# Third norm and router as one stage: half-wise choices, 16-bit places, shared down projection in the last stage

## The reference

```python
logits = x @ gate_weight.T                    # x: the normed tokens, 64 experts
scores = softmax(logits)
# the 3 best of 8 groups (by their maximum) stay, then the 6 best experts of a token
topk_w, topk_i = top_k(masked scores, 6)
# place of a choice in its expert = how many earlier choices took that expert
slot = flat * 96 + minimum(pos, 95)           # 96 places; late ones overwrite place 95
buf = zeros.at[slot].set(x[tok])              # rows gathered per expert
out = silu(buf @ Wg) * (buf @ Wu) @ Wd        # 64 experts, M = 176
y = sum of a token's 6 rows, weighted by topk_w
shared = silu(x @ Sg.T) * (x @ Su.T) @ Sd.T   # all tokens, MS = 352
result = residual + y + shared
```

## Time and profile before

| | before |
|---|---|
| median of 3 runs | 1584.75 us (1584.71 to 1588.64) |
| profiled execution | 1592.02 us, its span 1590.2 us |
| TensorE busy | 1389.2 us (87%) |
| VectorE busy | 1122.2 us (71%) |
| ScalarE busy | 677.8 us (43%) |
| GpSimd busy | 736.8 us (46%) |
| mean granted TensorE clock | 0.926 of 2.4 GHz |

### The profile page before, as it was taken

The page is one execution under the profiler, slowest core; times in us unless marked ns, Lnnn a source line. Parts: engine busy times, 40 slices in busy tenths (PEclk is TensorE's granted clock), DMA queues, the critical chain, the costliest instruction groups (busy, mean ns, idle before and its releaser), DMA issues. The chain is left out here.

```text
span 1590.2 us, 35116 instructions
## 1 busy us (share of the span) xinstructions
PE 1389.2 (87%) x13733; PEld 973.9 (61%) x13733; DVE 1122.2 (71%) x2131; ACT 677.8 (43%) x1430; POOL 736.8 (46%) x811
## 2 busy tenths in 40 slices
PE   3859999998669999999999999999986986799942
PEld 2424555555536777777777777777765545688831
DVE  4767888885767888888788888887864579122229
ACT  1226777772135555555555555555551110122200
POOL 0341111100228787666667666766650026577710
PEclk9968999999779999999999999999997698899965
DMA  3052000000016888798788878887882500599948
GB/s 107 1 221 98 2 2 2 2 2 1 29 59 137 155 153 146 136 159 142 143 141 155 149 138 143 155 145 138 147 144 76 175 1 3 172 291 286 269 128 267
DMA packets 423541, 191.57 MB, mean 120 GB/s; under 512 B 377506, under 2 KB 397696, under 8 KB 423248
## 3 DMA queue, kind: packets, MB, share of 16 engines
q1 hardware_dynamic: 404576, 164.08, 49.1%
q0 software_dynamic: 6144, 12.52, 2.8%
q10 hardware_dynamic: 12656, 12.72, 2.5%
HBM read 73.91 MB, written 23.13 MB: 61 GB/s over the span
## 5 line engine op out<-in xcount | busy, mean ns | idle before, releaser
L945 POOL CAST a_ph<-a_p 128x1024 f16<-128x1024 f32 (+7 forms) x256 | 247.6, 968 | 233.3 <-ACT a_p L1091 232.0
L1141 DVE TENSOR_TENSOR a_ph<-a_p,a_ph 128x1024 f16<-128x1024 f32 (+7 forms) x256 | 260.2, 1016 | 14.5 <-POOL a_ph L945 14.4
L1091 ACT ACTIVATE a_p<-bank,a_negm 128x1024 f32<-128x1024 f32 (+7 forms) x256 | 189.1, 739 | 124.8 <-DVE a_negm L1158 124.4
L1051 PE MATMUL bank<-a_v,a_pt 128*128 128x128 f16 x3456 | 234.7, 219 | 6.0 <-DMA a_pt<-a_ph 6.0
L1033 PE MATMUL bank<-a_k,a_q 128*128 128x512 f16 (+3 forms) x1152 | 229.1, 326 | 7.9 <-ACT a_p L1091 7.9
L1051 PEld LDWEIGHTS bank<-a_v,a_pt 128*128 128x128 f16 x3456 | 211.0, 98 | 37.0 <-issue 5.7
L1158 DVE TENSOR_REDUCE a_negm<-bank 128x1 f32<-128x1024 f32 (+7 forms) x256 | 189.8, 742 | 24.7 <-PE bank L1038 23.0
L976 PE MATMUL bank<-x_part,wsplit 128*128 128x512 f16 x768 | 189.1, 383 | 1.9 <-PEq L185 1.8
L690 ACT ACTIVATE a_p<-bank 128x1024 f32<-128x1024 f32 x192 | 153.0, 810 | 68.5 <-PE bank L575 57.6
L1033 PEld LDWEIGHTS bank<-a_k,a_q 128*128 128x128 f16 x1152 | 98.8, 98 | 69.3 <-ACT a_p L1091 8.9
L710 DVE TENSOR_REDUCE a_max<-bank 128x2 f32<-128x1024 f32 (+3 forms) x128 | 128.7, 1021 | 17.4 <-PE bank L575 14.9
(11 more groups left out here) (206 smaller groups left out, 2452.4 us busy)
## 6 DMA issues: line engine op xcount, KB each, us to landing
wgu<-in_wgu SPq DMA_DIRECT2D x64, 352.0 KB
choice_rows<-zero SPq DMA_DIRECT2D x24, 512.0 KB, 5.8
wh<-in_wqkv SPq DMA_DIRECT2D x32, 384.0 KB, 4.0
c_rows<-choice_rows ACTq DMA_DIRECT2D x16, 768.0 KB
wd<-in_wd SPq DMA_DIRECT2D x64, 176.0 KB
a_pt<-a_ph SPq DMA_TRANSPOSE x256, 3.8
x<-in_x SPq DMA_DIRECT2D x1, 2048.0 KB, 8.7
wo<-in_wo SPq DMA_DIRECT2D x1, 2048.0 KB, 10.0
```

The source lines that it names most:

```text
L945: pool.tensor_copy(halves[j][:, :, 0, :], probs[j % 2][:, 0:blocks[j] * P].rearrange("p (n q) -> p n q", q=P)).then_inc(h_ready, 1)
L1051: ins = pe.matmul(V_ps[j % 2][:, 0:DH1], turned[j][:, 2 * q + a, :], vs[n % 2][v_][:, q, :], start=(q == 0 and (a, v_) == PARTS[0]), stop= ...
L1091: act.activation(probs[j % 2][:, 0:w_], S_ps[j % 2].rearrange("p a n -> p (a n)")[:, 0:w_], ACT.Exp, bias=negm[:, n % 2, j:j + 1], accum_o ...
L1141: dve.tensor_tensor(halves[j][:, :, 1, :], probs[j % 2][:, 0:blocks[j] * P].rearrange("p (n q) -> p n q", q=P), halves[j][:, :, 0, :], ALU ...
```

## The change

The block of norm n3 is gone; its work is in the router block. TensorE turns two tiles, then logits and turns alternate (`logit(p)`, `turn(p)`); ScalarE alone copies to `xT`. The small loads are issued before the stores of `xn`, the weights behind them. `tmp`, `sc`, `msc` and `sg` lie in the memory of `xn`, so VectorE waits for the stores (`s_kept`) ahead of the softmax. Softmax, groups and choices run for 8 tiles at a time, on scores that are not yet divided by their sum. Tables of choices and places are f16 (`oh`, `mask`, `cm`, `posh`, `prod`, `fin`, `vh`); ScalarE copies the places to SBUF and makes the second half of `at_expert`; the running sum goes by groups of four tiles, finished by extra matmuls. Place 95 is no longer clipped but added by 16 small matmuls of `fin`. The gate and up steps 9 to 11 lie between the first picks. The shared down projection and its sum run in `combine`, in the same PSUM group as the rows of place 95.

```diff
-        with ExitStack() as c1:
-            g.xn = g.sb("xn", [P, NT, D], F32, c)
-            norm(nc, g, "n3", "keep")
...
+            for q in range(4):
+                sp.wait_ge(s_xn, 4 * q + 4)
+                sp.dma_start(xv[:, 4 * q:4 * q + 4, :], xn[:, 4 * q:4 * q + 4, :]).then_inc(s_kept, 16)
...
+            turn(0)
+            turn(1)
             pe.wait_ge(s_in, 80)
...
+            for p in range(NT // 2):
+                logit(p)
+                if p + 2 < NT // 2:
+                    turn(p + 2)
...
+            for n in range(9):
                 gate_up(n)
...
+            places()
+            gate_up(9)
+            pick(0)
+            gate_up(10)
+            pick(1)
+            gate_up(11)
+            pick(2)
+            pe.wait_ge(s_h, len(gu_steps))
             pe.wait_ge(s_wov, 1)
...
+            pick(3)
+
+            pe.wait_ge(s_fin, 1)
+            for t in range(NT):
+                pe.matmul(g.bank[0][0:C, 1, 0:E], lastcol[:, :], fin[:, t, :], start=False, stop=False)
+            pick(4)
+            pick(5)
...
+            for h in range(2):
+                act.wait_ge(s_sub, h + 1)
+                act.activation(sc[:, h * HT:h * HT + HT, :], tmp[:, h * HT:h * HT + HT, :], ACT.Exp).then_inc(s_ex, 1)
...
+            dve.wait_ge(s_kept, 64)
+            shifted(0)
+            groups(0)
+            choices(0)
+            shifted(1)
+            shared(1)
+            groups(1)
+            shared(2)
+            choices(1)
+            shared(3)
+            eid = iotah[:, 0:E].unsqueeze(1).to_broadcast([P, NT, E])
+            for k in range(K):
+                dve.tensor_tensor(oh[:, k], eid, gih[:, :, k:k + 1].to_broadcast([P, NT, E]),
+                                  ALU.is_equal).then_inc(s_oh, 1)
+                dve.wait_ge(s_oh, k + 1)
+                if k:
+                    chained(dve.tensor_tensor(mask[:, :, :], oh[:, 0] if k == 1 else mask[:, :, :], oh[:, k], ALU.add))
+                shared(min(4 + k, 7))
...
+            def slots(k):
+                if k == 0:
+                    dve.wait_ge(s_posh, 2)
+                chained(dve.tensor_tensor(prod[:, :, :], posh[:, :, :], oh[:, k], ALU.mult))
+                chained(dve.tensor_reduce(v[:, k, :], prod[:, :, :], AX.X, ALU.add))
+                chained(dve.tensor_copy(vh[:, k, :], v[:, k, :]))
+                if k >= 2:
+
+                    dve.wait_ge(s_used, k - 1)
+                dve.tensor_tensor(ph[k % 2][:, :, :], iotah[:, :].unsqueeze(1).to_broadcast([P, NT, C]),
+                                  vh[:, k, :].unsqueeze(2).to_broadcast([P, NT, C]), ALU.is_equal).then_inc(s_ph, 1)
...
-                shared_sum(2 * k)
-                shared_sum(2 * k + 1)
...
+            shared(10)
+            slots(1)
+            shared(11)
+            slots(2)
+            shared(12)
+            dve.wait_ge(s_sel, 1)
+            dve.scalar_tensor_tensor(msc[:, :, :], pos, C - 1.5, sc[:, :, :], ALU.is_gt,
+                                     ALU.mult).then_inc(s_wov, 1)
+            slots(3)
+            slots(4)
+            slots(5)
...
-                pool.tensor_scalar(eh[k % 2][:, :, 1, :], oh[:, k], float(k + 1), None, ALU.mult).then_inc(s_eh, 1)
...
+                for m in range(NMS):
+                    w_ = SM[m][1]
+                    pe.matmul(b_, g.hT[0:w_, m, t * P:(t + 1) * P], g.sd[0:w_, m, :], start=(m == 0), stop=False)
+                if t == 0:
+                    pe.wait_ge(s_l, 16)
+                pe.matmul(b_, g.wovT[:, t * P:(t + 1) * P], last[:, :], start=False, stop=True).then_inc(s_mm, 1)
```

More of the change, by code:

```diff
@@ new lines, in pick @@
+            def pick(k):
+                pe.wait_ge(s_e0, k + 1)
+                pe.wait_ge(s_e1, k + 1)
+                pe.wait_ge(s_ph, k + 1)
+                for t in range(NT):
+                    ins = pe.matmul(g.bank[0][0:C, 1, 0:2 * E], ph[k % 2][:, t, :],
+                                    eh[k % NEH][:, t, :, :].rearrange("p a e -> p (a e)"),
+                                    start=(k == 0 and t == 0), stop=(k == K - 1 and t == NT - 1))
+                ins.then_inc(s_used, 1)
@@ L1529, in shared @@
                     done += 1
+            for t in range(NT):
+                dve.bn_aggr(mv[:, t, :], g.stats[:, t, :]).then_inc(s_ag, 1)
+            dve.wait_ge(s_ag, NT)
+            chained(dve.tensor_copy(g.mean[:, :], mv[:, :, 0]))
+            chained(dve.tensor_copy(t1[:, :], mv[:, :, 1]))
+            chained(dve.tensor_scalar(ve[:, :], t1[:, :], EPS, None, ALU.add))
+            dve.wait_ge(s_sq, 1)
+            chained(dve.reciprocal(sq[:, :], sq[:, :]))
+            chained(dve.tensor_tensor(t1[:, :], sq[:, :], sq[:, :], ALU.mult))
@@ L1531, in _ @@
+            chained(dve.tensor_tensor(t1[:, :], t1[:, :], ve[:, :], ALU.mult))
+            chained(dve.tensor_scalar(t1[:, :], t1[:, :], -0.5, 1.5, ALU.mult, ALU.add))
+            chained(dve.tensor_tensor(g.rstd[:, :], sq[:, :], t1[:, :], ALU.mult))
+            for t in range(NT):
+                dve.tensor_scalar(xn[:, t, :], g.x[:, t, :], g.mean[:, t:t + 1], g.rstd[:, t:t + 1],
+                                  ALU.subtract, ALU.mult).then_inc(s_xn, 1)
             dve.wait_ge(s_in, 80)
[L1532 removed]
@@ new lines, in _ @@
+            slots(0)
+            dve.wait_ge(s_pos, 3)
+            chained(dve.tensor_scalar(cnt[:, :], count, -1.0, None, ALU.add))
+            chained(dve.tensor_tensor(fin[:, :, :], posh[:, :, :], cnt[:, :].unsqueeze(1).to_broadcast([P, NT, E]),
+                                      ALU.is_equal))
+            dve.nop().then_inc(s_eq, 1)
+            shared(10)
[6 more added lines that the diff above has]
+                                     ALU.mult).then_inc(s_wov, 1)
```

341 lines of the change are left out of this document (191 added, 150 removed).

## The result

| | before | after |
|---|---|---|
| median | 1584.83 us (1584.71 to 1588.64, 4 runs) | 1559.75 us (1558.85 to 1561.75, 4 runs) |
| ratio | | 0.9835, 95% interval 0.9818 to 0.9852 |
| profiled execution | 1592.02 us, span 1590.2 | 1561.75 us, span 1559.2 |

The account below looks back on a forecast made before the run. No engine bounds the stage from normed tiles to the source-list cast, a relay; the experts wait on that cast. Its legs put the cast 29.7 us earlier: 1584.75 - 29.7 = 1555.0 us, range 1546 to 1569.

Parts of the forecast that it names:

- Leg 1: Norm and logits: TensorE ends at 1239.3 instead of 1246.4 us, and VectorE gets the first half's Exp at 1238.6.
- rival of the logits at 2.4 GHz: Mixing turns and logits lifts TensorE's clock, so the relay starts some 7 us earlier: 1548 us; chance 0.05.
- Leg 2: First half's groups and choices: 9.3 us, then an added wait for Exp, table load and Silu; first product ends at 1251.3.
- rival that they cost more: Both ScalarE table loads, now on the path, cost up to 1.7 us more: 1556.7, or 1557.8 with drains; chance 0.10.
- Leg 3: Second half's groups and choices on VectorE: 9.3 us, reaching the one-hot tables at 1260.6.
- Leg 4: One-hot compares and gate and up steps, paced by TensorE at 3.43 us a step; sums by groups end at 1279.6.
- Leg 5: Places and picks, 4.0 us a choice, the first two stretched by GpSimd; cast at 1317.5 instead of 1347.2 us.
- factor of 1.7: Stretch of VectorE's at_slot compares at full overlap with GpSimd, adding 1.5 and 1.3 us to the first two choices.
- they would halve: Rival: compares with all operands 16-bit take half the time, saving 5.7 us: 1549.3 us; chance 0.15.
- The last stage: Takes the shared down projection's 96 records; TensorE's 6.7 us a pair of tiles against VectorE's 5.4, costed at 0.
- rival that TensorE becomes the bound: In the last stage, TensorE's clock stays low to the end, adding 2.9 us: 1557.9 us; chance 0.10.
- The slower rival: TensorE stays at 1.2 GHz through the router, 6.9 us a step: 1586.5 us, chance 0.04; half of it 1569, 0.08.

Follow-up runs that it names:

- before_again: The kernel before, timed and profiled once more without an edit: median 1589.59 us, ratio 0.9998 to before.
- after_again: The changed kernel, timed and profiled once more without an edit: median 1559.56 us, ratio 0.9803 to before.
- whole: The changed kernel with softmax, groups and choices run once over 16 tiles instead of twice over 8: median 1554.50 us, ratio 0.9775 to before.
- places_f32: The changed kernel with the table of places and its product with each choice in float32: profiled once at 1561.90 us.
- early_exp: The changed kernel with ScalarE's first-half Exp moved ahead of its copies of the last two pairs of tiles: median 1556.09 us, ratio 0.9798 to before.
- late_tokens: The changed kernel with GpSimd's first four token products held back until the mask is summed: median 1564.83 us, ratio 0.9843 to before.
- down_alone: The kernel before with only the shared down projection and its sums moved to the last stage: profiled once at 1589.01 us.
- fed_warm: whole with VectorE's shared products spread between group and choice steps, plus 60 needless matmuls around the last two picks: median 1558.20 us, ratio 0.9795 to before.
- norm_apart: The changed kernel with the third norm in a block of its own again: profiled once at 1566.28 us.
- early_both: early_exp with VectorE's maxima and subtraction of the second half's logits moved ahead of the first half's choices: median 1555.62 us, ratio 0.9792 to before.

## Why the prediction was right, and where its steps were not

The total held: 29.4 us of the stage for 29.7, and 1561.75 us for 1562.3 on the profiled execution. The 4.75 us between 1555.0 and the measured 1559.75 are the choice of base: I took the gain off before's median of three, while its 15 runs beside before_again show that the profiled execution belonged to the commoner kind. Taken off the median of those 15 the same 29.7 give 1561.2, against 1559.56 of after_again beside them. Under the total, step by step (us behind the first normed tile, forecast and measured):

| | forecast | measured |
|---|---|---|
| first half's Exp to VectorE | 22.1 | 20.4 |
| first product ends | 34.8 | 33.3 |
| first one-hot compare | 44.1 | 42.6 |
| seventh product ends | 56.5 | 55.5 |
| sums end | 63.1 | 62.2 |
| slots(0) starts | 66.4 | 65.5 |
| slots(1) ends | 78.9 | 80.5 |
| masked scores end | 87.7 | 87.6 |
| last compare ends | 99.7 | 99.2 |
| cast | 101.0 | 101.3 |

**Leg 1** was sized 1.7 us too long, TensorE's part of it 3.4 (22.8 for 19.4). From the earlier trace rows four turns and eight logit records cost 2.76 us; in the mixed stream they took 2.45 (a cycle of after, at the low clock), 2.5 us in eight. The granted clock, which I kept at 0.50 to the end, rose at about 1232 (0.55 over 1215.5 to 1234). The rival of the logits at 2.4 GHz is a matter of degree: in whole and places_f32 the clock rose 7 us sooner, by their windows at about 10.5 us behind the first normed tile and not 17.5, and `gate_up(0)` with it by 3.3 and 3.5. What I didn't see at all is that the stage no longer hangs on TensorE there, but on the order on ScalarE: early_exp takes 4.8 us out of this leg with one move.

**Leg 2** had its length right (12.7 forecast, 12.9 measured from Exp to product) and the added wait in place, 2.60 on VectorE. TensorE's gap ahead of `gate_up(2)` was 6.82 and not 2.6, as it reached the gap sooner and at 7.08 us for two steps. Both table loads are 1.28 us, and the Silu starts 0.01 us behind the second one, so the rival that they cost more is out. The Trainium skill (ScalarE: Activation LUTs, What ACT_TABLE_LOAD costs) adds a drain of 1.38 us to each switch; no row of after, nor of early_exp, has it on the path.

**Leg 3** was 9.3, as forecast.

**Leg 4** is where the reason failed: "paced by TensorE". The step was 3.57 us of VectorE, not 3.43 of TensorE, as late_tokens shows. The sign that I had named, TensorE steps of 3.43 from the fourth on, came true (Silus at 1264.63, 1268.07 and 1271.50) and proves nothing, since TensorE kept its own step a little ahead while VectorE never waited for it. I had its compares at 1.27 with 0.5 us for GpSimd in all; they took 2.49 and three times 2.20. That is 4.2 us above the undisturbed time, hidden in my sum by a pace that I gave to another engine and that is nearly the same. With VectorE's burden lightened alone only 1.7 us come out, as TensorE stands right behind.

**Leg 5** ended right by errors that met: slots(0) took 6.1 us for 5.5 and slots(1) 7.3 for 5.3 (2.05, 3.41 and a cast of 0.50 beside GpSimd). In turn VectorE did not wait for step 10, for which I had kept some 1.8 us: pick(0) took 1.56 and the step 4.88, not 1.9 and 6.2, and the legs before had 0.9 in hand. The last pick was 1.91 at the low clock, behind 2.42 us of idle, so the cast stood 2.1 us behind the last compare and not 1.2. The factor of 1.7 was misread twice. The mean of 2.49 in the earlier trace rows is not of six compares while GpSimd worked: two of them took 1.76, so the other four averaged 2.86, a factor of 1.6. And it is no factor: it is waiting time, and depends on when the GpSimd instruction ends. The compares took 1.21 and 1.76 with all operands 16-bit, which was the value chosen; that they would halve is out, and so the rule of the Trainium skill on a repeated element (Vector Engine (DVE) Microarchitecture Reference, 5.1 Performance modes) holds by the row at 1312.22. The sign against me, that GpSimd's products stretch more than two choices, came just true: the cast of the third took 0.74 instead of 0.17.

**The last stage** came out at no cost, with less to spare than I thought: TensorE starts 8.2 us ahead of VectorE, and a pair of tiles costs it 8.0 us at the low clock, where I had 6.7 from the earlier trace rows (0.40 us a record there, 0.48 here; the twelve of the earlier trace rows were not all at the low clock, it was 0.92 over their last 0.7 us), and 4.2 at the high one, where I had half of 6.7. VectorE's 5.4 lie between. The rival that TensorE becomes the bound decided at 6.3 a pair; it is out only because the clock rose in the third tile (in down_alone in the fifth). With a low clock to the end, eight pairs of 8.0 from 1504.96 would end 13 us behind VectorE's last addition (an estimate), not my 2.9.

**The slower rival** needed eight steps at the low level. After had one behind the long gap (6.0 us from its start to its Silu) and one partly low behind pick(0) (4.88); the other stops of 2 to 3 us left the steps at 3.6 to 3.7. In other executions it was other steps: 9 and 11 in fed_warm, at 5.04 and 5.13.

What I counted wrongly without harm is the 6.0 us of removed sums. down_alone shows them to be worth nothing by themselves. That they and the removal of L1632 are one gain, not two, is argued from it and not tried.

## What to carry to other kernels

When stages are merged so that halves can overlap, look at every engine's queue for what stands between the first half's two steps: here the Exp behind copies undid most of the overlap, and moving one instruction brought 4.8 us by the marks. Work that is taken from one engine beside another pays only if the other isn't the pace, and two paces within 5% of each other hide a wrong reason behind a right sum. A two-input product on GpSimd costs VectorE nothing while it runs reductions or instructions with a PSUM operand; beside casts and instructions with two SBUF inputs it does. And before a difference of 1 to 3 us between two profiles is given to an edit, see whether the low clock fell on the same instructions.

## What the runs showed of the hardware

**VectorE waits out a GpSimd instruction.** Beside GpSimd's two-input products VectorE's two-input instructions in SBUF end a fixed time behind the end of GpSimd's: a compare of 1.22 becomes 2.20 to 2.49, one of 1.76 becomes 3.41, a product of 0.68 becomes 2.05 to 2.27, and a cast of 128x16, otherwise 0.17, becomes 0.50 to 1.59. That it is waiting is seen in whole, where three compares start later under L1741 and take 1.35, 1.49 and 1.62: all end 1.08 us behind the end of GpSimd's instruction, as those of after do. f16 is not spared. Reductions (1.22) and products with a PSUM operand (0.69) run on unchanged. The Trainium skill (GPSIMD Engine Reference, 8. Key points) names VectorE instructions with two SBUF inputs and those in a 2-port mode as the ones in contention; the rows agree on two inputs, and show the price: the rest of GpSimd's instruction, whatever the size of the one that waits. Which mode the cast runs in, no row shows. Under GpSimd's one-input L1605 it is less: a product of 1.22 took 2.05 and ended 0.66 us ahead of it. GpSimd pays too: its product of 1.90 took 2.41 when VectorE had begun first.

**The granted clock is not the same in every execution.** In the stream of turns and logits it rose to 1.0 at 17.5 us behind the first normed tile in after and at 10.5 in whole, with TensorE busy without a gap ahead of it in both. Behind gaps of about 3 us ahead of the same step it fell to 0.50 in both profiles of before and not in down_alone. A stage with such a stretch varies by 3 us for this alone, and two profiles of it are only comparable from the far side of it on. Further on, the low stretch falls on `pick(0)` and step 10 in after, whole and early_exp and on `pick(1)` and step 11 in norm_apart and early_both, which is 1.6 us at the cast.
